# A second token tile in the feed-forward loop, and the constant added in the next attention

## The reference

```
xn = layernorm(x)
q1, q2 = split(xn @ Wq.T);  k1, k2 = split(ctx @ Wk.T);  v = ctx @ Wv.T      # 16 heads, 8 key heads, 32 wide
attn = softmax(q1 @ k1.T) @ v - lam * softmax(q2 @ k2.T) @ v
x = x + (rms_norm(attn) * g * (1 - LAMBDA_INIT)) @ Wo.T
h = layernorm(layernorm(x)) * ln1_g + ln1_b                                   # the feed-forward part has its own norm
h = gelu(h @ ternary(w1).T + b1)                                              # 512 -> 2048
h = layernorm(h) * ln2_g + ln2_b
x = x + h @ ternary(w2).T + b2                                                # 2048 -> 512
```

## Time and profile before

| what | before |
|---|---|
| median of 3 runs | 2364.73 us |
| profiled execution, whole | 2363.08 us |
| its span, first to last instruction | 2361.3 us |
| mean granted clock of TensorE | 0.957 of full |
| PE, DVE, ACT, POOL busy | 91%, 75%, 64%, 45% |
| chain that ended last | PE 45%, POOL 25%, DVE 17% |

### The profile page before, as it was taken

One profiled execution on the slowest core, in us unless ns is written; L12 is line 12 of the kernel. 1 busy time (PEld: TensorE's weight loads), 2 busy tenths in 40 slices (PEclk: granted clock), 3 DMA queues, 4 the chain that ended last, 5 costly groups with the idle time before them and its releaser, 6 DMA issues.

```text
span 2361.3 us, 45358 instructions
## 1 busy us (share of the span) xinstructions
PE 2159.8 (91%) x18239; PEld 1197.7 (51%) x18239; DVE 1775.6 (75%) x2700; ACT 1521.4 (64%) x1973; POOL 1053.3 (45%) x803
## 2 busy tenths in 40 slices
PE   7767999999999999999999999999999999999888
PEld 5344454554555455455555555555555555455443
DVE  4676878686887868688786868778686877868673
ACT  3566676666667675666767566676756667675654
POOL 2301717346191734618173461807346180734516
PEclk9868999999999999999999999999999999999899
DMA  8414122130413213031331313132140323212010
GB/s 295 110 44 85 47 82 63 36 89 23 115 47 87 58 42 86 20 99 47 85 75 43 89 20 96 47 90 55 42 106 19 96 46 91 54 42 68 2 55 18
DMA packets 253009, 160.15 MB, mean 68 GB/s; under 512 B 171813, under 2 KB 221581, under 8 KB 252289
## 3 DMA queue, kind: packets, MB, share of 16 engines
q1 hardware_dynamic: 249792, 152.07, 24.8%
q0 software_dynamic: 3008, 5.20, 0.7%
HBM read 51.82 MB, written 20.38 MB: 31 GB/s over the span
## 4 chain that ended last, share of the span: by engine, by line
PE 45%; POOL 25%; DVE 17%; ACT 6%; issue 5%; DMA 2%; SPq 1%; POOLq 0%; DVEq 0%; ACTq 0%
POOL attn_raw L683 23%; PE ps L1615 10%; PE ps L1597 5%; PE ps L1532 4%; PE ps L1447 3%; PE ps L1448 3%; PE ps L1449 3%; PE ps L1636 2%; PE ps L1561 2%; DVE arena L1117 2%; ACT arena L868 2%; PE ps L1562 2%; DVE attn_raw L1147 2%; PE ps L1560 2%; PE ps L1537 2%
## 5 line engine op out<-in xcount | busy, mean ns | idle before, releaser
L683 POOL TENSOR_TENSOR attn_raw<-attn_raw 128x512 f32<-128x512 f32 x448 | 628.0, 1421 | 46.9 <-ACT attn_raw L839 20.4
L1597 PE MATMUL ps<-rows,w1T 128*128 128x512 f16 x2048 | 485.5, 380 | 9.0 <-DVE rows L1238 9.0
L661 POOL TENSOR_TENSOR q<-q 128x512 f16<-128x512 f32 x128 | 196.2, 1537 | 661.0 <-ACT q L798 644.1
L1117 DVE TENSOR_REDUCE arena<-ps 128x6 f32<-128x924 f32 (+1 forms) x330 | 350.5, 1082 | 46.1 <-PE ps L1500 44.3
L1615 PE MATMUL ps<-w2T,arena 128*128 128x512 f16 x1440 | 344.9, 395 | 0.0
L1243 DVE SCALAR_TENSOR_TENSOR arena<-attn_raw,vec_cols,arena 128x512 f16<-128x512 f32 x256 | 305.1, 1196 | 36.1 <-ACT arena L837 36.0
L834 ACT ACTIVATE attn_raw<-ps,vec_cols,wstep 128x512 f32<-128x512 f32 x256 | 199.0, 777 | 202.3 <-PE ps L1597 199.2
L1597 PEld LDWEIGHTS ps<-rows,w1T 128*128 128x128 f16 x2048 | 193.7, 98 | 229.9 <-DVE rows L1238 21.3
L650 POOL TENSOR_TENSOR rstd<-var,neghalf 128x4 f32<-128x4 f32 x48 | 48.6, 1013 | 477.7 <-DVE var L1188 365.9
L1147 DVE TENSOR_TENSOR attn_raw<-arena,attn_raw 128x1024 f16<-128x1024 f32 (+1 forms) x128 | 199.4, 1588 | 53.9 <-ACT attn_raw L814 51.6
L807 ACT ACTIVATE arena<-ps 128x1024 f32<-128x1024 f32 x128 | 130.8, 1022 | 169.1 <-PE ps L1532 169.0
(11 more groups left out here) (192 smaller groups left out, 4496.5 us busy)
## 6 DMA issues: line engine op xcount, KB each, us to landing
stack_raw<-q SPq DMA_DIRECT2D x744, 64.0 KB, 2.0
arena<-in_x SPq DMA_DIRECT2D x64, 256.0 KB, 2.8
out<-arena SPq DMA_DIRECT2D x64, 256.0 KB, 2.3
arena<-in_x SPq DMA_DIRECT2D x14, 1024.0 KB, 5.4
arena<-in_L_ffn_w SPq DMA_DIRECT2D x7, 1024.0 KB, 16.4
rows<-in_x SPq DMA_DIRECT2D x2, 1024.0 KB, 7.6
stack_raw<-in_L_xattn_Wq SPq DMA_DIRECT2D x8, 256.0 KB, 10.1
k_att<-k_store SPq DMA_DIRECT2D x4, 495.0 KB
```

The source lines that it names most:

```text
L683: ins = pool.tensor_tensor(acc[:, e, :], acc[:, e, :], src[:, j % NG, :], ALU.add)
L1117: dve.tensor_reduce(negmax[:, tt:tt + 2, u0:u1], ps[:, bank:bank + 2, 0:(u1 - u0) * S].rearrange("p b (u s) -> p b u s", s=S), AX.X, ALU.m ...
L1597: ins = pe.matmul(ps[:, B_H + j % 2, :], w1T[:, k, j * P:(j + 1) * P], rows16[:, e, k, :], start=(k == 0 and e == 0), stop=(k == KD - 1 an ...
```

## The change

Four things change, none of them arithmetic apart from the order in which three terms are added to x_res.

- For blocks 1 to 14 the loop sums token tiles 0 and 1, in banks 2 and 3; only tiles 2 and 3 stay late. For block 0 tile 1 stays late, since bank 3 is in use there (output_vectors). Block 15 is as before.
- The constant is added by POOL in the next attention, at z, after the tile's shift; SP's store waits for it and add_ffn no longer does. Block 15 keeps it where it was.
- POOL's second power_half comes ahead of the low half of query 4.
- Block 0: FIRST is another order. The bias product comes before the scores, w2's tiles 10 to 15 get their signs and transposes behind the attention, and the attention's transposes and the stacking of the first query pair move between those of the weights.

```
-FIRST = tokens("r1 w0 s0 l0 b0 w1 s1 l1 x1 w2 q0 ... w4 ... l3 w5 t0 q1 s4 v2 l4 w6 w7 s5 v3 l5 w8 t1 q2 s6 v4 l6 w9 w10 "
-               "s7 v5 l7 q3 w11 v6 t2 w12 v7 w13 w14 w15")
+FIRST = tokens("r1 w0 b0 s0 l0 w1 s1 x1 l1 w2 q0 ... w4 ... l3 w5 t0 q1 s4 v2 l4 w6 s5 v3 l5 w7 w8 t1 q2 u12 u13 s6 v4 l6 "
+               "w9 u14 u15 s7 v5 l7 q3 v6 t2 v7")
+SIGNED_IN_FIRST = 10
...
+        def loop_banks(c):
+            return (2, 3) if c else (2,)
...
 def store(c, tt):                                   # SP
     wait(sp, s_out, c, TT, tt + 1)
+    wait(sp, s_const, c, TT, tt + 1)
...
-                    for p, (n0, n1) in enumerate(((0, 9), (9, 12))):
+                    for p, (n0, n1) in enumerate(((0, 6), (6, 9), (9, 10))):
                         for n in range(n0, n1):
                             transpose_ternary(JH + n)
                         transpose_attn(0, p)
-                        if p == 0:
+                        if p == 1:
                             stack_queries(1, 0, 0)
...
+                else:
+                    for n in range(SIGNED_IN_FIRST, JH):
+                        transpose_ternary(JH + n)
...
-            def add_constant(c, tts):               # POOL
-                wait(pool, s_xhat2, c, TT, TT)
+            def add_constant(c, tt):
+                if c == NBLK - 1:
+                    wait(pool, s_xhat2, c, TT, TT)
+                else:
+                    wait(pool, s_out, c, TT, tt + 1)
...
+                    elif what == "z" and i:
+                        add_constant(i - 1, n)
...
                 power_half(i, 0)
+                power_half(i, 1)
                 if ahead:
                     q_lo(i + 1, QATT)
-                power_half(i, 1)
...
-                if i:
-                    add_constant(i, range(TT))
+                if i == NBLK - 1:
+                    for tt in range(TT):
+                        add_constant(i, tt)
...
             def add_ffn(c, tt, bank):               # DVE
-                wait(dve, s_const, c, TT, tt + 1)
+                if c == NBLK - 1:
+                    wait(dve, s_const, c, TT, tt + 1)
...
-                    elif (what, n) in LATE and i:   # PE
+                    elif (what, n) in LATE and i and (what == "h" or i == 1):
...
-                        ffn_step(i - 1, n, (2,))
+                        ffn_step(i - 1, n, loop_banks(i - 1))
...
-                banks = (2,) if ahead else range(TT)
+                banks = loop_banks(i) if ahead else range(TT)
```

More of the change, by code:

```diff
@@ L85 @@
 POOL_PROLOGUE = tokens("q0 q1 p0 q2 q3 p1 q4 q5 p2 q6 q7 p3")
-FIRST = tokens("r1 w0 s0 l0 b0 w1 s1 l1 x1 w2 q0 s2 v0 l2 w3 w4 s3 v1 l3 w5 t0 q1 s4 v2 l4 w6 w7 s5 v3 l5 w8 t1 q2 s6 v4 l6 w9 w10 "
-               "s7 v5 l7 q3 w11 v6 t2 w12 v7 w13 w14 w15")
+FIRST = tokens("r1 w0 b0 s0 l0 w1 s1 x1 l1 w2 q0 s2 v0 l2 w3 w4 s3 v1 l3 w5 t0 q1 s4 v2 l4 w6 s5 v3 l5 w7 w8 t1 q2 u12 u13 s6 v4 l6 "
+               "w9 u14 u15 s7 v5 l7 q3 v6 t2 v7")
+SIGNED_IN_FIRST = 10
 ROUNDED_AHEAD, SIGNS_AHEAD = 3, 2
@@ L558, in iteration @@
                         transpose_attn(0, p)
-                        if p == 0:
+                        if p == 1:
                             stack_queries(1, 0, 0)
-                    transpose_attn(0, 2)
                     load_x_in(2)
-                    for n in range(12, JH):
-                        transpose_ternary(JH + n)
                 else:
@@ L662, in q_lo @@
                                    ALU.subtract).then_inc(s_q_lo, 1)
-            def add_constant(c, tts):
-                wait(pool, s_xhat2, c, TT, TT)
+            def add_constant(c, tt):
[3 more added lines that the diff above has]
+                    wait(pool, s_out, c, TT, tt + 1)
                 if c == 0:
                     pool.wait_ge(s_rows, 2)
-                for tt in tts:
-                    pool.tensor_tensor(x_res[:, tt, :], x_res[:, tt, :], out_const[:], ALU.add).then_inc(s_const, 1)
+                pool.tensor_tensor(x_res[:, tt, :], x_res[:, tt, :], out_const[:], ALU.add).then_inc(s_const, 1)
             def sum_gelu(c, j):
@@ L691, in iteration @@
                     elif what == "g" and i:
-                        if i == 1:
-                            add_constant(0, range(TT))
                         power(3, s_gln, s_rstd4, i - 1)
+                    elif what == "z" and i:
+                        add_constant(i - 1, n)
                     elif what == "q" and ahead:
@@ L893, in iteration @@
                 attn_hi(i, KD - 1)
+                if i == 0:
+                    for n in range(SIGNED_IN_FIRST, JH):
+                        ternary_sign(JH + n)
                 load_table(ACT.Gelu)
@@ L1292, in iteration @@
                         attn_lo(i, n)
-                    elif what == "w" and n + ROUNDED_AHEAD < JH:
+                    elif what == "w" and n + ROUNDED_AHEAD < 12:
                         ternary(JH + n + ROUNDED_AHEAD)
+                    elif what == "u":
+                        ternary(JH + n)
                     elif what == "b":
```

## The result

| what | before | after |
|---|---|---|
| median of 4 runs (range) | 2364.29 us (2363.55 to 2365.78) | 2326.64 us (2323.63 to 2329.56) |
| ratio, 95% interval | | 0.984 (0.9823 to 0.9857) |
| span of the profiled execution | 2361.3 us | 2321.8 us |
| mean granted clock of TensorE | 0.957 | 0.952 |
| PE, DVE, ACT, POOL busy | 91%, 75%, 64%, 45% | 93%, 74%, 65%, 44% |

The kernel is 37.7 us faster, with 69 forecast. In the changed kernel L1597, L1625, L1636, L1532 and L1447 of before are L1612, L1640, L1651, L1547 and L1462; VectorE's L1117, L1238, L1243 are L1129, L1250, L1255; GpSimd's L683, L656, L670 are L691, L662, L678; ScalarE's L809, L814 are L818, L823.

A forecast was written before the change was run, and what follows sets the result against it. TensorE, busy 2159.8 of 2361.3 us, was taken as the bound. Terms 35 + 11 - 10 + 22 + 11 = 69 us gave 2295 (chance 0.60), own range 2280 to 2312, with A and B 2265 to 2335.

The forecast's parts named there:

- sign of being wrong: Blocks staying at 135 us or more, explained by waits of first scores and query products, or VectorE's attention share reaching its whole length.
- The second tile in the loop: Tile 1's matmuls join the loop in blocks 1 to 14: 2.5 us a block, 35 us; bounds 0 and 4.6 a block.
- as a middle: Block boundary: GELU sums plus first scores, without the late matmuls, take 4.1 us to the query product, 11.2 before.
- PE waits some 1.5 us: Block boundary: the second query product waits for the first one's bank, which ScalarE reads after its copies.
- the shorter wait should shorten the slow stretch: Block boundary: less idle PE before the sums means less time at 1.2 GHz; used to choose 4.1 us.
- The power: Second half's RMS power runs once its variances are ready: 1.5 us for each of 15 blocks, 22 us; bounds 10 and 30.
- it moves up by only 1.1: ScalarE's scaled high half behind its query copies, late next after the power; the 0.48 us wait before first hidden product moves too.
- The constant: Four additions leave the loop's head, gaining 11 us (0.8 a block), and enter the attention, costing 10 us (0.7 a block).
- The first block: Block 0's attention transposition issues earlier, waits of 7.53 and 3.40 us go: 11 us; bounds 3 and 14.
- A: Rival: the late product was only cover, its removal opens equal waits, the 35 us go: 2331 us; chance 0.20.
- B: Rival: the clock holds with the shorter wait and VectorE's terms fall well: 2267 us, 2238 at the extreme; chance 0.14.
- C: Rival: additions make VectorE the attention's bound, decided once it loses over 3.2 us there: slower, 2402 us; chance 0.06.

The follow-up runs named there:

- e7: Changed kernel with ScalarE's scaled high half of the rows ahead of its copy of query 6 instead of behind: 2296.61 us, ratio 0.9714.
- e3: Changed kernel with all four additions of the constant back at the head of the loop, before the first accumulation: 2331.84 us, ratio 0.9851.
- e5: Changed kernel with the first block's orders, weights' signs and transposes as before the change: 2337.4 us, ratio 0.9886.
- e12: e11 with five more unused matmuls where PE waits between first scores and query product: 2269.4 us, ratio 0.9596.
- e8: Changed kernel with six unused 512-column matmuls just before the GELU sums of blocks 1 to 14: 2312.78 us, ratio 0.9783.
- e1: Changed kernel with token tile 1 summed late again in every block, the other three parts kept: 2340.29 us, ratio 0.9889.
- e9: e1 with thirteen unused matmuls in PE's wait before the GELU sums: 2303.23 us, ratio 0.9744.
- e11: e7 with the six unused matmuls of e8 before the GELU sums: 2291.75 us, ratio 0.9692.

## Why the prediction was right in its direction and too large

The measured 2326.64 us lies in the range of 2265 to 2335, which takes in the rivals, and outside the forecast's own, 2280 to 2312. The prediction's sign of being wrong, blocks that stay at 135 us or more, came true with 135.05, and so did the waits that it named for this case.

**The second tile in the loop: 35 us forecast, 11.6 measured. This is the term that failed.** Its first half held: the sums come 0.8 us later (2.0 less the 0.8 of the constant's head was forecast) after a wait of 1.3 us (1.7). The step that failed is the 4.1 us from sums to query product, taken "as a middle" (the terms' own bounds, 1.9 to 3.4 and 1.3 to 2.4, have theirs at 4.5). It was 967.49 - 961.46 = 6.0, and 6.3 on the mean of 14 blocks. I had looked for the late wait of ScalarE at the second query product ("PE waits some 1.5 us") and had not seen that the first one too writes a bank that the first exponentials read; the late product had covered it. It costs 21.6 us in 13 times. The second half of the same step, "the shorter wait should shorten the slow stretch", failed as well: from sums to fourth scores PE is at 1.2 GHz for 8.4 us a block on the mean, with 7.8 before, and the new gap lies in this stretch. That less idle time keeps the clock better, which the prediction drew from two boundaries, did not hold in after. So the query product starts 4.4 us nearer to T0 (before 990.75 - 927.32 = 63.4, after 59.0), but takes 3.9 us instead of the 2.6 at full clock, and the wait foreseen for the second query product never came because its turn is now later. The copy of the row maxima ended at 959.40, T0 + 51.0, where 52.4 was forecast, and from block 1 on the only wait for their landing is one of 0.35 us. From sums to fourth scores this leaves 2.05 of the 4.5.

**The power: 22 forecast, 14.2 measured.** The mechanism was right, the size was not: "it moves up by only 1.1" had the wait at T0 grow from 0.48 to some 0.8, and it is 1.4 to 1.5 (22.1 / 15). The order on ScalarE, the high half behind a query copy that waits for GpSimd, was the next bound, as e7 shows.

**The constant: +11 and -10 forecast, +2.6 in sum measured.** Both terms were too large. At the head VectorE's split is back at 0.75 us, and PE's wait for the maxima fell from 1.45 to 0.51 in the block shown; but e3 shows that hardly any of it reaches the end. In the attention VectorE does pay. The timeline of DVE, after, with two of GpSimd's additions at 992.76 to 996.69 beside the second group:

```profile
987.88 2.88 DVE L1159 TENSOR_TENSOR attn_raw<-arena,attn_raw 128x1024 f16<-128x1024 f32 x2
...
994.15 4.16 DVE L1159 TENSOR_TENSOR p<-arena,p 128x1024 f16<-128x1024 f32 x2
```

The second group in the timeline of DVE, before:

```profile
1016.12 2.89 DVE L1147 TENSOR_TENSOR p<-arena,p 128x1024 f16<-128x1024 f32 x2
```

The pair takes 4.16 us beside them and 2.89 without. In the 35 us that answer to the earlier trace rows VectorE is busy for 32.81 us, after:

```profile
987.00:1022.00 35.00, 33.12 (x468) 20.46 (x466) 32.81 (x47) 23.52 (x24) 10.27 (x6) 1.00 0.48 128
```

It had 3.2 us free and has 2.2: the loss was taken from its idle time. PE's part from fourth scores to transposes grew by 0.22 us on the mean, in the inner blocks but one by nothing (3.3 us in all at most, 10 charged). The Trainium skill ("SBUF — State Buffer", Who interferes with whom) calls the port pair that the two engines share an exclusive lock and has the loser blocked for the whole operation. For a pair beside two additions this would be 2 x 1.35 us if VectorE always lost; the rows show 4.16 - 2.89 = 1.27 for it. GpSimd lost as well: its two additions take 3.93 us here, and one alone at 999.95 takes 1.27. Together the two engines lose 2.7 us, about the length of the two additions, as if the blocking were divided between them. That is read from one pair and not tested.

**The first block: 11 forecast, 10.2 in the trace and 10.9 by e5.** The wait of 7.53 us is gone, and SyncE issues the first attention transposition at 173.54 instead of 186.75. Of the exponentials' waits in the first block 3.48 us remains as the longest.

**The rivals.** A, the lost cover, gave 2331 and comes nearest to the time, and its mechanism is half of the truth: there is a new wait for exponentials of about a third of the late product's length. But the tile isn't worth nothing, and the time is near A's only because the power fell short and the attention cost less. B, the clock holds, did not happen by itself; e12 makes it happen in large part and stands where B stood (2269.4, with 2267 given), though by work that the change doesn't have and with e7's order, so that the two figures agree by chance. C did not occur: VectorE lost 1.0 us between the marks where over 3.2 decide.

**In one sum** of the misses: tile -23, power -8, constant's head and attention together +2, first block 0: -29 to -30 of the 31 us missing. How much of the tile's miss is the wait of the query product and how much the clock was not separated. The traces show both, e12 fills the wait and raises the clock at once, and a run that gives the query product another bank, and nothing else, was not made.

## What to carry to other kernels

When an instruction is taken out from between two others, list the semaphore waits of the next one too, bank by bank: what it waits for was hidden by the instruction removed, and the first wait that came up here was that of the very next instruction. Where a matmul engine has a gap of a microsecond or two ahead of work that sets the end, price the clock behind the gap as well as the gap, and try matmuls with unused results in it; here eleven a block, with one exchange of order on ScalarE, gave 58 us of 2327. When a wait is removed, read which instruction is next on the releasing engine and what that one waits for: here half of the gain came back there, and one moved copy freed it.

## What the hardware showed that I had not expected

- Unused matmuls in a gap pay. Six of 512 columns a block made the kernel 13.5 us faster (e8), thirteen made e1 34 us faster (e9), and five more in a second gap another 23 us (e12). The Trainium skill ("TensorE: Matmul & The Clock Gate", What's actually happening) says that the throttled state is the default and activity releases it; e9 agrees, with a mean clock of 0.83 in the 10 us from the first scores on instead of e1's 0.70.
- A shorter gap alone did not keep the clock: with 1.30 us idle ahead of the sums instead of 3.34 the mean of those 10 us was 0.62 (after) instead of 0.70 (e1). After has the second gap of 1.65 us within them. With the first gap filled and the second left PE is at 1.2 GHz for 6.4 us between sums and fourth scores (e11), with both filled for 2.3 (e12). The second gap alone was not filled in any run.
- The sixteen one-column fp32 matmuls of the sums take 1.95 us at the first level and up to 3.58 at the second (e1), so a lowered clock costs in the sums themselves too.
- Moving one copy behind another on ScalarE (e7) gave 29.8 us where the wait it removed accounts for some 21. The other 8 lie in the slow stretch half a block later, which is 1.1 us shorter; what links the two is open.
